# Order of the ramp: both head groups' queries ahead of the convolution, the later weights' transfers behind their copies, the second roots ahead of a copy, all queries ahead of the keys

## The reference

```
layer 0, for each image (1024 rows of 256 channels)
  q       = layernorm(x) @ wq + bq
  o       = gelu(depthwise 7x7 convolution, stride 2, of q as an image of channels)
  offsets = tanh(1x1 convolution of o to 2 channels)        -> 256 sampling positions
  interp  = bilinear samples of x at these positions         (256 rows)
  k = v   = interp @ wv + bv
  qh, kh, vh = heads(q @ mq_w), heads(k @ mk_w), heads(v @ mv_w)   (8 heads of 32, with biases)
  att     = softmax(qh kh^T) vh
  z       = att @ mo_w + mo_b + x
  y       = gelu(layernorm(z) @ mlp_w + mlp_b) + z
layer 1, for each image of y
  theta, phi, g = projections to 32, 32 and 128 channels; phi and g pooled by 2x2 maxima
  out     = y + sigma * (softmax(theta phi^T) g @ w_o + b_o)
```

## Time and profile before

| | us |
|---|---|
| median of 3 runs | 514.39 (514.14 to 515.91) |
| the profiled execution | 512.36 |
| its span between first and last instruction | 510.6 |
| mean granted clock of TensorE | 0.98 |
| busy: PE, DVE, ACT, POOL | 454.9, 286.2, 211.6, 120.1 |

### The profile page before, as it was taken

The page is one execution under the profiler, slowest core; times in us unless marked ns, Lnnn a source line. Parts: engine busy times, 40 slices in busy tenths (PEclk is TensorE's granted clock), DMA queues, the critical chain, the costliest instruction groups (busy, mean ns, idle before and its releaser), DMA issues.

```text
span 510.6 us, 9319 instructions
## 1 busy us (share of the span) xinstructions
PE 454.9 (89%) x3743; PEld 318.8 (62%) x3743; DVE 286.2 (56%) x609; ACT 211.6 (41%) x338; POOL 120.1 (24%) x163
## 2 busy tenths in 40 slices
PE   6788979988989999989899999989899897888956
PEld 5657756645567576656686666656767564665735
DVE  4518446846673367667754345567546647625433
ACT  1122212545346045655333336745173664662230
POOL 5420301167003001681002003761030030100000
PEclk9999989989999999999999999999999998999978
DMA  7298866581947930293157801472226200000202
GB/s 211 76 168 171 163 101 126 85 169 65 137 69 99 233 54 3 85 124 64 42 101 103 164 3 46 90 111 27 83 42 86 83 3 2 1 2 2 82 2 83
DMA packets 30489, 42.90 MB, mean 84 GB/s; under 512 B 6075, under 2 KB 21230, under 8 KB 30446
## 3 DMA queue, kind: packets, MB, share of 16 engines
q1 hardware_dynamic: 23598, 34.82, 37.4%
q0 software_dynamic: 3584, 4.50, 3.8%
q10 hardware_dynamic: 3264, 2.99, 2.9%
HBM read 16.16 MB, written 4.19 MB: 40 GB/s over the span
## 4 chain that ended last, share of the span: by engine, by line
PE 57%; DVE 13%; DMA 10%; POOL 7%; issue 5%; ACT 5%; SPq 1%; ACTq 0%; DVEq 0%; POOLq 0%
PE ps_d L759 8%; PE ps_d L884 5%; PE ps_d L861 5%; PE ps_d L961 5%; PE ps_d L747 4%; PE ps_s L808 4%; DMA xa<-in_x_dram 4%; PE ps_v L850 4%; DMA corners<-in_x_dram,row_of 3%; PE ps_v L844 3%; PE ps_t L827 3%; PE ps_d L779 3%; POOL samp L1937 3%; DVE mx L1613 3%; PE ps_d L903 2%
## 5 line engine op out<-in xcount | busy, mean ns | idle before, releaser
L1226 ACT ACTIVATE prob<-ps_t 128x1024 f32<-128x1024 f32 x64 | 65.4, 1021 | 95.8 <-PE ps_t L827 92.2
L1613 DVE TENSOR_REDUCE mx<-ps_s 128x4 f32<-128x1024 f32 x64 | 78.2, 1222 | 24.1 <-PE ps_s L808 23.2
L1909 POOL DMA_DIRECT2D q_st<-mx_t x64 | 34.0, 532 | 244.0 <-ACT mx_t L1218 226.0
L759 PE MATMUL ps_d<-cstack,conv_w 128*32 128x256 f32 x1024 | 59.0, 380 | 3.4 <-issue 1.8
L808 PE MATMUL ps_s<-k_st,q_st 96*128 96x256 f32 x256 | 49.9, 317 | 8.2 <-DVE mx L1613 7.1
L759 PEld LDWEIGHTS ps_d<-cstack,conv_w 128*32 128x32 f32 x1024 | 36.3, 108 | 23.9 <-issue 6.2
L808 PEld LDWEIGHTS ps_s<-k_st,q_st 96*128 96x128 f32 x256 | 35.9, 191 | 20.5 <-DVE mx L1613 12.6
L827 PE MATMUL ps_t<-q_st,k_st 98*128 98x256 f32 x256 | 42.6, 289 | 6.2 <-ACT zt L1285 3.0
L827 PEld LDWEIGHTS ps_t<-q_st,k_st 98*128 98x128 f32 x256 | 35.5, 192 | 8.9 <-issue 5.1
L1627 DVE TENSOR_TENSOR att<-ps_v,rden 128x256 f32<-128x256 f32 x32 | 13.6, 424 | 43.2 <-ACT rden L1237 43.2
L844 PE MATMUL ps_v<-prob,vh 128*32 128x256 f32 x512 | 35.1, 392 | 1.5 <-DVE att L1627 1.5
(11 more groups left out here) (178 smaller groups left out, 744.7 us busy)
## 6 DMA issues: line engine op xcount, KB each, us to landing
q_st<-q_parts SPq DMA_DIRECT2D x42, 256.0 KB, 5.6
xa<-in_x_dram SPq DMA_DIRECT2D x8, 512.0 KB, 9.6
z_all<-in_x_dram SPq DMA_DIRECT2D x8, 512.0 KB, 7.9
out_dram<-z_all SPq DMA_DIRECT2D x8, 512.0 KB, 2.6
cstack<-qpad SPq DMA_DIRECT2D x22, 180.5 KB, 5.7
k_st<-cstack SPq DMA_DIRECT2D x22, 128.0 KB, 4.2
q_st<-z_all SPq DMA_DIRECT2D x6, 256.0 KB, 5.7
cstack<-att SPq DMA_DIRECT2D x6, 180.5 KB, 9.8
```

What stands on the lines that cost most here:

```text
L759: ins = pe.matmul(ps[32 * k:32 * k + 32, 0, :], conv_w[:, cb * 4 + k, y, x, :], cstack[:, cb, k, y:y + HG_, x:x + WG_], start=n == 0, stop ...
L1226: drain(act.activation(prob[:, u % 2, 2 * pr:2 * pr + 2].rearrange("p h m s -> p (h m) s"), ps_t[:], ACT.Exp), t_ring, "t", b, u, pr)
L1613: drain(dve.tensor_reduce(mx[:, u % 2, half, :], ps_s[:], AX.X, ALU.max), s_ring, "s", b, u, half)
```

## The change

It reorders instructions in the ramp of all engines; none is added or removed, and no tile changes.

1. DVE: of the second half's four statistics, two go behind the first half's `row_shift`.
2. ACT: the roots of image 0's second half go ahead of the wait for PE and of the copy of the turned `wq`.
3. PE, ACT, DVE: the queries of head group 1 for image 0's first half go from behind the offsets to ahead of the convolution, right behind those of group 0.
4. SP: the copies of these queries' parts, six transfers, go ahead of the issue of `for_rest`.
5. PE, ACT: the queries of group 1 for the second half go ahead of the keys. DVE: their conversions go, one ahead of the second half's sampling, one behind it and ahead of the keys' low parts.
6. The list of the banks' uses follows.

```diff
--- before.py
+++ after.py
@@ -128,9 +128,9 @@
 def dense_order():
 
     order = [("qimg", 0, cb, jp) for jp in range(2) for cb in range(CB)]
-    order += [("qh", 0, 0, 0)] + [("conv", 0, cb) for cb in range(CB)] + [("off", 0), ("qh", 0, 0, 1)]
-    order += [("qimg", 1, 1, jp) for jp in range(2)] + [("qimg", 1, 0, 0), ("qh", 0, 1, 0), ("kh", 0)]
-    order += [("qh", 0, 1, 1), ("qimg", 1, 0, 1), ("conv", 1, conv_halves(1)[0])]
+    order += [("qh", 0, 0, hg) for hg in range(NHG)] + [("conv", 0, cb) for cb in range(CB)] + [("off", 0)]
+    order += [("qimg", 1, 1, jp) for jp in range(2)] + [("qimg", 1, 0, 0), ("qh", 0, 1, 0), ("qh", 0, 1, 1)]
+    order += [("kh", 0), ("qimg", 1, 0, 1), ("conv", 1, conv_halves(1)[0])]
     for b, s in slots():
         n, m, mm = b + 1, b - 1, b - 2
         cur, post, fin = b < B, 0 <= m < B, 0 <= mm < B
@@ -644,9 +644,9 @@
             stack_conv(0, 0)
             stack_conv(0, 1)
             load_a(1)
-            for_rest.start(sp)
             stack_q(0, 0, [0])
             stack_q(0, 0, [1])
+            for_rest.start(sp)
             stack_conv(1, 1)
             stack_k(0)
             stack_conv(1, 0)
@@ -1069,21 +1069,19 @@
             setup_vectors()
             setup_query_bias()
             pe.wait_ge(setup_act, A_QUERY)
-            queries(0, 0, [0])
+            queries(0, 0)
             pe.wait_ge(setup_pool, P_CONV)
             conv(0, 0)
             pe.wait_ge(setup_pool, P_CONV + 1)
             conv(0, 1)
             setup_key_bias()
             offsets(0)
-            queries(0, 0, [1])
             q_image(1, 1)
             q_image(1, 0, [0])
             setup_values()
-            queries(0, 1, [0])
+            queries(0, 1)
             pe.wait_ge(setup_act, A_ALL)
             keys(0)
-            queries(0, 1, [1])
             q_image(1, 0, [1])
             conv(1, conv_halves(1)[0], STEPS_OF_1[0])
 
@@ -1374,7 +1372,6 @@
             def setup_queries():
                 act.wait_ge(setup_pe, 1)
                 setup_copy(t_wqt, ps_s[:, 0:2, :])
-                row_deviation(0, [1])
                 for_fused.wait(act)
                 heads_inside(t_mqp, t_mq)
 
@@ -1397,6 +1394,7 @@
             for_fused.start(act)
             act.wait_ge(setup_pool, P_EPS)
             row_deviation(0, [0])
+            row_deviation(0, [1])
             setup_queries()
             for_keys.start(act)
             for cb in range(CB):
@@ -1406,21 +1404,19 @@
                 stack_planes(act, 0, cb, (2, 3))
             setup_weights()
             act.wait_ge(setup_dve, D_QUERY_BIAS)
-            query_hi(0, 0, [0])
+            query_hi(0, 0)
             row_deviation(1)
             conv_gelu(0, 0)
             conv_gelu(0, 1)
             offset_tanh(0)
-            query_hi(0, 0, [1])
             setup_values()
-            query_hi(0, 1, [0])
+            query_hi(0, 1)
             act.wait_ge(setup_dve, D_BIAS)
             key_hi(0)
             for hg in range(NHG):
                 act.wait_ge(k_hi_done.sem, k_hi_done.at(0, hg + 1))
                 act.dma_start(k_st[32:64, 0, :, hg, :].bitcast(F32), k_parts[:, 0, hg, :].bitcast(F32)
                               ).then_inc(k_in[hg].sem, 16)
-            query_hi(0, 1, [1])
             for b, s in slots():
                 slot(b, s)
             tail(B - 1)
@@ -1855,8 +1851,9 @@
             row_moments(0, first)
             for_norm.wait(dve)
             row_scale(0, first)
-            half_stats(0, second)
+            half_stats(0, second[:2])
             row_shift(0, first)
+            half_stats(0, second[2:])
             row_moments(0, second)
             row_norm(0, second)
             setup_orders()
@@ -1869,7 +1866,7 @@
             setup_columns()
             setup_query_bias()
             dve.wait_ge(setup_dve, D_QUERY_BIAS)
-            query_lo(0, 0, [0])
+            query_lo(0, 0)
             bias_row_parts(mlpb_hl, mlpb_all, BIAS_EMPTY)
             row_stats(1)
             row_scale(1, range(NT))
@@ -1878,17 +1875,16 @@
             setup_key_bias()
             for_q.wait(dve)
             positions(0)
-            query_lo(0, 0, [1])
             corner_weights(0)
             q_image(1, 1)
             q_image(1, 0, [0])
             sampled(0, 0)
+            query_lo(0, 1, [0])
             sampled(0, 1)
-            query_lo(0, 1, [0])
+            query_lo(0, 1, [1])
             dve.wait_ge(setup_dve, D_BIAS)
             key_lo(0)
             setup_values()
-            query_lo(0, 1, [1])
             q_image(1, 0, [1])
             for b, s in slots():
                 slot(b, s)
```

## The result

The changed kernel takes 518.75 us (median of 7 runs, 515.46 to 520.9), the kernel before, run beside it, 515.57 (512.53 to 516.81). The ratio is 1.0077, with a 95% interval of 1.0043 to 1.0112: 0.8% slower, where 1.3% faster was forecast. The profiled execution took 519.62 us (span 517.8) against 512.36 (span 510.6).

The account below looks back on a forecast made before the run. The start of the loop's first scores on PE was taken as the bound; the ramp's steps moved it from 76.5 to 70.0 us, 6.5 us off the median 514.39, giving 507.9 us, range 506.0 to 512.4.

Parts of the forecast that it names:

- Part 1: Second half's roots and statistics early in the ramp: PE's second products at 17.2 instead of 20.49, 3.3 us gained.
- Part 2: Both head groups' queries ahead of the first convolution, which starts at 28.5 to 28.7, 3.0 us earlier.
- hole (c): PE's idle 1.76 us ahead of 40.42, at the second convolution's start, supposedly a code fetch; 0 to 3.5, 1.8 kept.
- Part 3: SP's queue: copies take 4 to 5 us off the gather's stretch; image 1's rows at 37.6, positions at 47.0.
- late rows: Rival: queries' copies delay image 1's rows to 42.4, positions to 51.4; 2.0 us gained, 512.4; chance 0.14.
- Part 4: Positions to keys: DVE's conversion, not the gather, is late next; keys start at 61.7, end at 63.6, 6.1 us earlier.
- Part 5: All queries ahead of the keys, worth 0 to 0.9 us; scores 6.3 us after the keys, at 69.9 to 70.0.
- The loop as a rigid block: From the first scores to the end of the span: the distance stays 434 us, so the end moves with the start.
- The slower rival: SP's issue of weights slips by more than 5 us and they land during the gather; 515 to 518, chance 0.06.

Follow-up runs that it names:

- roots_only: The kernel before with only the second half's roots ahead of the copy and the split statistics; 511.38 us, ratio 0.9923.
- sp_old: The changed kernel with SP issuing the weights' transfers ahead of the queries' copies again, as before the change; 512.37 us, ratio 0.9944.
- both_late: The changed kernel with the queries' copies behind the stacking of image 1's planes and the weights in slot 3 of image 0; 511.01 us, ratio 0.9915.
- xa_steps: xa_first with nine instead of six steps of image 1's convolution ahead of the first scores; 509.74 us, ratio 0.9892.
- keys_first: sp_old with group 1's queries of the second half put behind the keys again on PE, ACT and DVE; 512.27 us, ratio 0.993.
- xa_first: both_late with the load of image 1's rows issued ahead of the planes' copies; 510.23 us, ratio 0.9888.
- w_late: The changed kernel with the weights' transfers moved out of the ramp to slot 3 of image 0; 519.29 us, ratio 1.0096.
- xa_ramp: sp_old with the load of image 1's rows issued ahead of the planes' copies; 511.97 us, ratio 0.9923.
- half_q: The changed kernel with group 0's three queries' copies ahead of the weights and group 1's three behind them; 514.96 us, ratio 0.9986.
- xa_ramp_steps: xa_ramp with nine instead of six steps of image 1's convolution ahead of the first scores; 513.84 us, ratio 0.9951.

## Why the prediction was wrong, step by step

**Part 1** held: second products at 17.50 (17.2 forecast), and roots_only gives it 4 us by itself. PE's first products began at 13.12 and not 12.9, because the load of `wq` into PE waited for its transfer, which the sum left out.

**Part 2** held up to the convolution, 28.51 (28.5). The step that failed is its last sentence: hole (c), which the prediction says it "cannot price in the new order", was left as a term of 0 to 3.5 us, and the sum kept one hole of 1.8. That one measured 2.09. But the term was of the wrong kind: it stood for one hole of a given size, and not for a fetch that depends on what is queued. The change put six copies of 256 KB ahead; so a second packet of the instruction queue, which before had come unnoticed at 41.5 in the earlier trace rows's second convolution, came at 46.5, and PE stood still for 4.76 us. Its consequence, the lower clock, was left out with it: from the end of the convolution to the positions it took 3.8 us (50.84 to 54.67), against 2.2 before. The 7.7 us between the 47.0 forecast and 54.67 are 4.8 of the second hole, 0.3 of the first, 1.6 behind the convolution, and 1.0 of the convolution's own records behind the first hole (four more of them stood there, and the last six ran at the lower clock).

**Part 3** counted the copies' time only against the two transfers that it knew to be awaited, the rows of image 1 and the gather. Image 1's rows were there at 39.67, 2.1 us behind the 37.6 of equal shares. DVE ended their shift at 48.60 (45.35 + 3.25), before PE ended the convolution (50.84), so this cost nothing here. But it was hidden by the hole: an estimate from sp_old's 7.59 us for the same 133 records and the usual 2.2 us behind them puts PE's way without the hole at 47.5, and then DVE would have been late by about 1 us. The rival "late rows" was half true, and its price was only covered by a larger one.

**Part 4** held in its mechanism: the conversion (68.14 to 68.89) and not the gather came last before the second sampling; hole 1.83 us (1.8 forecast), keys 1.97 us (1.9), at full clock. The 4 to 5 us that the copies were to take from the gather were mis-sized: from its last issue's end to its last data it is 8.2 us before, 6.5 in sp_old and 6.6 in both_late, so 1.7 us at most. That a hole of about 2 us leaves the clock up held in the changed kernel and not in sp_old, whose keys took 2.50 us behind a hole of 2.33.

**Part 5** was mis-sized: the keys' copies took 7.5 us from the end of the keys to the scores (72.83 to 80.34), not 6.3. PE's hole there is 3.0 us, and behind it the clock fell: 3.07 us for the value rows, 1.89 in xa_steps. The lower clock that part 4 avoided was met one step later. keys_first shows that with SP's old order nothing of the part reaches the end.

**The loop as a rigid block** was wrong. Behind a start that came 5.3 us earlier, sp_old waits for another transfer, the rows of image 2:

```profile
DVE st L1469 <- DMA xa<-in_x_dram: 2.4, 1, 2.4
```

Its positions of image 2 are at 95.82, 3.1 us earlier than before, and its end 3.2 earlier. So about 2 us of the ramp's gain went there. In the changed kernel the loop added 3.3 us. 1.5 of them came by the clock behind the scores, up to the positions of image 2. From these the chain of work runs over the gather and the copies of queries to the products of L871, which start at 151.95 instead of 146.33, 5.6 us later. PE had a hole of 3.86 us ahead of them, and behind it the clock fell: the image products that follow took 3.23 us instead of 1.74, and the lag became 7.3 and stayed so.

**The slower rival** had the right sign and the wrong mechanism: the weights ended their issue at 50.3, before the gather began at 56.1.

## What to carry to other kernels

A hole of PE that the profile puts down to no wait, at a time when transfers fill the DMA engines, is not noise to be carried along: look for packets of the instruction queue near its end, and treat the code of a long unrolled stretch as one more transfer that a reorder of the others can delay (that the packets are code stays an inference here; that the order of the copies moves packet and hole is shown). Before a bulk transfer is moved ahead of such a stretch, compare with a version that moves it behind: here the two orders of SP differ by 1.3% with all else equal. And a hole filled in front of one step pays only if it does not open in front of the next: here the keys kept the upper clock, and the value rows took 3.07 us instead of 1.89.

## What the runs showed of the hardware

The instruction queue's packet was moved at 38.5 to 39.5 us with no queries' copies ahead of it (both_late; in sp_old the first was issued at 38.68), at 44.0 with three and the weights behind them, and at 46.5 with six, with or without the weights, PE being at the same point of its program (its convolution went on at 37.4 to 38.0 in all five kernels). When the fetch is asked for, no row shows, nor which part of the path holds it. The Trainium skill, DMA: Bandwidth & Descriptors, section "Queues, rings and completion order", says that each DMA engine takes the queue rows that have work in turn, switching at packets; by that a request would pass a long queue on another row within a few packets. The dose seen here does not look like it, unless the request itself was made late.

In the kernels before and changed the level of the clock fell behind holes of 3.96, 4.76, 3.0 and 3.86 us and not behind those of 2.82, 2.09 and 1.83. But it fell behind 2.39 us in xa_first (value rows 3.34 us), 2.34 in w_late and 2.33 in sp_old, and not behind 3.04 in xa_ramp (1.89 us). It fell even behind 1.82 us in half_q and 1.54 in xa_ramp_steps, there 2 to 3 us after PE had gone on: half_q's hole ends at 46.95, and the granted clock is 1.00 in 48 to 49 us and 0.50 in 50 to 51. From 1.5 to 3 us the length of the hole alone did not decide.
